# Cross-attention of a perceiver layer on one core: scores in two passes over the key columns, queries turned in 32 x 32 blocks by VectorE and spread by ScalarE, context in two banks

## The chip, the core and the metric

One core of one Trainium2 chip runs the whole kernel as one launch. Its engines are TensorE (PE in the views; its weight loads are PEld), VectorE (DVE), ScalarE (ACT), GpSimd (POOL) and SyncE (SP, which here only issues DMAs). The metric is device time in microseconds. Before the change it is 833.94 us, the median of three runs (831.2 to 836.29).

## The reference, cut to what matters

The layer has a cross-attention, a self-attention with relative positions, and a block with a second self-attention and a mixture of experts. The change touches the first alone. With x of 16 batches x 64 queries x 512 features, and 1,601 keys a batch, all in fp32:

```
h = layernorm(x)                                   # per query row, no scale or shift
scores  = einsum('bsh,bqh->bsq', ctx, h)           # 1601 keys x 64 queries
context = einsum('bsq,bsh->bqh', softmax(scores, axis=1), ctx)
y = x + context
```

## The kernel before

**Tiles.** The 16 batches are done two at a time, in `NT` = 8 tiles of 128 rows (64 queries of each of two batches; `b` is 0 or 1). The keys of a batch lie in `nat[k % 2]` with keys in the partitions, as 12 full groups of 128 and a tail of 65 (`JM` = 12, `TAIL` = 65, `JT` = 13). `nat` has two buffers, so the keys of tile k + 2 are loaded over those of tile k, in four pieces (`PIECES`: groups 0 to 3, 4 to 7, 8 to 11, the tail). SyncE issues each when a semaphore `context_part` says that the context product no longer needs the old ones (L476).

**Scores.** The product needs features in the partitions, on both sides. VectorE turns the keys in blocks of 32 x 32 (`columns`, L1808) into `ctxT`: partition group i of 32 holds keys 32i to 32i + 31 of each 128-key group, and the 512 features are 16 blocks `j`. A tile has two parts, `PARTS`: key groups 0 to 7 (`h` = 0, 8 turns of 128 x 1024) and 8 to 12 (`h` = 1, 8 turns of 128 x 640). Each turn counts `columns_ready` up. `scores(k)` (L583) then runs, for each of 16 blocks j, for both batches and all four partition groups, one product of 32 rows, 64 columns of queries and up to 416 keys (`KEYS_IN`), accumulated over j into PSUM banks 0 to 3 (`scores4`). In fp32 a product is two matmul instructions with a weight load each: 256 matmuls and 256 loads a tile. It waits chunk by chunk (`c`) for `columns_ready` of the second part of the keys.

**Queries.** As each partition group needs all queries, ScalarE writes the normed row four times over (`queries`, L1391, 128 x 2048 into `qn`), TensorE transposes it in 16 products (`query_transposes`, L548), four to a bank (`QUERY_BANK`), and ScalarE copies the four banks into `q4` (`query_columns_out`, L1396). This is woven into the previous tile's work.

**Softmax and context.** VectorE takes maxima (`maxima`, L1797), ScalarE exponentials (`exps`, L1400) into `prob`, TensorE transposes them (`prob_transposes`, 13 for a tile in four fills f, into `PROB_BANK`), VectorE copies fill 0 out and ScalarE fills 1 to 3 (`probs_out`). `context(k, f)` (L611) multiplies them with `nat`, f for f, all into bank 7: 16 matmuls for f below 3, four for the tail. VectorE's `finish` (L1853) scales bank 7 and adds it to y, and the next tile's context waits for it (`y1_ready`).

**Order.** It is written by hand, on each engine. On TensorE (L636 to L659) one turn of the loop is: scores(k), context(k-1, 2 and 3), prob_transposes(k, 0), query_transposes(k+1, 0), prob_transposes(k, 1), query_transposes(k+1, 1 and 2), context(k, 0), query_transposes(k+1, 3), prob_transposes(k, 2), context(k, 1), prob_transposes(k, 3). On VectorE (L1884 to L1898): maxima(k), first chunk of the next keys, finish(k-1), copy of fill 0, chunks 1 to 3, statistics for the later norm, denominators, the second part of the keys, then the first norm of tile k + 2 (`first_norm`: one statistic over 512 features and 15 small instructions). On ScalarE (L1436 to L1450): exponentials, the copies out, then `queries(k + 2)`.

Tile 0 is different: its keys 8 to 11 go through TensorE's transposes (`plain_key_transposes`, `plain_scores`), its score product has at most 288 columns (`FIRST_KEYS`), and its pieces are loaded in an order of their own (`load_first`, L452).

Of the kernel before, what the change touches and what calls it, by code (L numbers as in the profile page):

```python
# [17 lines left out]
P = 128  # L18
# [13 lines left out]
PROB_BANK = [4, 5, 4, 6]  # L32
# [10 lines left out]
PARTS = [(0, 8), (8, JT)]  # L43
NG, GB, NH, F, SEQ = 8, 8, 8, 128, 16
# [84 lines left out]
def perceiver_kernel(nc, x, ctx_keys, consts, vecs, rows, Wq, Wv, Wr, Wout, Wkvd, Wqd, Wku, Wqu, Wvu, Wropeq, Wropek,  # L129
                     Wo, Wexp, Wrouter, out):  # L130
    with ExitStack() as ctx:
# [60 lines left out]
        scope.close()  # L192

# [219 lines left out]
        def evicted(k):  # L413

            return 4 * k + (1 + HC if k > 0 else 0)
# [24 lines left out]
        def _(sp):  # L440
# [11 lines left out]
            def load_first():  # L452
# [5 lines left out]
                sp.dma_start(y[:, 1, :], x[P:2 * P, :]).then_inc(x_loaded[0], 16)  # L458
# [12 lines left out]
            sp.dma_start(y[:, 2:NT, :], x[2 * P:TOK, :].rearrange("(k p) d -> p k d", p=P)).then_inc(x_loaded[1], 16)  # L471
# [7 lines left out]
            sp.wait_ge(context_part, 3 * (NT - 1))  # L479
# [67 lines left out]
        def _(pe):  # L547
            def query_transposes(k, f):  # L548
                pe.wait_ge(qn_ready, k + 1)
                if f == 2:  # L550
                    pe.wait_ge(qt_act, evicted(k) + 1)
                elif k == 1 and f == 3:
                    pe.wait_ge(qt_act, evicted(1) + 2)
                elif k > 1 and f == 1:
                    pe.wait_ge(probT_dve, k)
                elif k > 1 and f == 3:
                    pe.wait_ge(probT_act, 3 * (k - 1) + 1)
# [25 lines left out]
            def scores(k):  # L583
                pe.wait_ge(qt_act, evicted(k) + 4)
                keys_in = FIRST_KEYS if k == 0 else KEYS_IN
                for c in range(HC):
                    pe.wait_ge(columns_ready, FIRST_COLUMNS + 16 * (k - 1) + 8 + 2 * c + 2 if k > 0 else 3 + HC + 2 + 2 * c + 2)
                    for j in range(4 * c, 4 * c + 4):
                        for b in range(2):
                            for i in range(4):  # L590
                                rows_i = slice(B32 * i, B32 * (i + 1))
                                last = nc.tensor.matmul(scores4[64 * b:64 * b + 64, i, 0:keys_in[i]],  # L592
                                                        q4[rows_i, j, 64 * b:64 * b + 64],
                                                        ctxT[rows_i, b, j, 0:keys_in[i]], start=j == 0, stop=j == NB - 1,
                                                        skip_group_check=True)
                last.then_inc(scores_full, 1)

            def prob_transposes(k, f):
# [3 lines left out]
                elif f >= 2 and k < NT - 1:  # L602
                    pe.wait_ge(qt_act, evicted(k + 1) + f)
                elif f == 2:
                    pe.wait_ge(probT_dve, k + 1)
                for j in range(4 * f, min(4 * f + 4, JT)):
# [4 lines left out]
            def context(k, f):  # L611
                if f == 0:
                    pe.wait_ge(probT_dve, k + 1)
                    if k > 0:
                        pe.wait_ge(y1_ready, k)
                    else:
                        pe.wait_ge(prob_ready, 3)
# [4 lines left out]
                for j in range(4 * f, min(4 * f + 4, JT)):  # L622
                    n = P if j < JM else TAIL
                    for b in range(2):
                        last = nc.tensor.matmul(bank[7][64 * b:64 * b + 64, :], probT[0:n, j, 64 * b:64 * b + 64],  # L625
                                                nat[k % 2][0:n, b, j, :], start=j == 0, stop=j == JT - 1,
                                                skip_group_check=True)
                if f != 2:
                    last.then_inc(context_part, 1)
# [6 lines left out]
            for k in range(NT - 1):  # L636
                scores(k)
                if k > 0:
                    context(k - 1, 2)
                    context(k - 1, 3)  # L640
                if k == 0:
# [3 lines left out]
                if k > 0:  # L645
                    query_transposes(k + 1, 0)
                prob_transposes(k, 1)
                if k > 0:
                    query_transposes(k + 1, 1)
                    query_transposes(k + 1, 2)  # L650
                context(k, 0)
                if k > 0:
                    query_transposes(k + 1, 3)
                prob_transposes(k, 2)
                context(k, 1)
                prob_transposes(k, 3)
# [4 lines left out]
            def norm_transposes(k):  # L661

                pe.wait_ge(hn_ready, k + 1)
                if k == 1:
# [725 lines left out]
        def _(act):  # L1390
# [4 lines left out]

            def query_columns_out(k, f):  # L1396
# [3 lines left out]
            def exps(k):  # L1400
                act.wait_ge(nmax_ready, k + 1)
                keys_in = FIRST_KEYS if k == 0 else KEYS_IN
# [33 lines left out]
            for k in range(NT - 1):  # L1436
# [4 lines left out]
                if k > 0:  # L1441
                    query_columns_out(k + 1, 0)
                probs_out(k, 1)
                if k > 0:
                    for f in range(1, 4):
                        query_columns_out(k + 1, f)
                probs_out(k, 2)
                probs_out(k, 3)
                if k + 2 < NT:
                    queries(k + 2)  # L1450
# [318 lines left out]
        def _(dve):  # L1769
# [44 lines left out]
            def first_columns():  # L1814
# [21 lines left out]
                first_factors(1, 2)  # L1836
# [16 lines left out]
            def finish(k):  # L1853

                dve.wait_ge(context_part, 3 * (k + 1))
                dve.scalar_tensor_tensor(y[:, k, :], bank[7][:], rinv[:, 0:1], y[:, k, :], ALU.mult,
# [26 lines left out]
            first_columns()  # L1883
            for k in range(NT - 1):  # L1884
                maxima(k)
                keys_columns(k + 1, 0, (0,))
                if k > 0:
                    finish(k - 1)
                probs_out(k)
                keys_columns(k + 1, 0, (1, 2, 3))  # L1890
                if k > 0:
                    second_stats(k - 1)
                denominators(k)
# [3 lines left out]
                if k + 2 < NT:  # L1897
                    first_norm(k + 2, k + 3)  # L1898
# [37 lines left out]
            dve.wait_ge(qt_full, turns(NT - 1) + 4)  # L1936
# [566 lines left out]
```

## Time and profile before

| | |
|---|---|
| median of three runs | 833.94 us |
| profiled execution | 833.91 us, span 832.1 us |
| granted TensorE clock, mean | 0.993 |
| PE busy (matmuls) | 793.4 us, 95% |
| PEld busy (weight loads) | 582.3 us |
| DVE, ACT, POOL busy | 521.0, 311.5, 301.2 us |
| read from and written to HBM | 102.0 and 24.2 MB, 152 GB/s over the span |

Busy time of an engine is the union of its instructions; matmuls overlap each other and their ends are modelled, so the chain of waits, which gives each moment to one instruction, is the better measure of what a group costs. "issue" in a view is idle time that ended with no semaphore the profile can name. The queue called "instruction" in the list of DMA queues carries the engines' own code.

### The profile page before, as it was taken

The numbers are of one execution on the slowest core, as the hardware profiler recorded it, in microseconds if no ns is written. First come the engines' busy times: TensorE is split into PE (matmuls) and PEld (weight loads), VectorE is DVE, ScalarE is ACT, GpSimd is POOL, SyncE is SP. The second block draws the span as 40 slices with busy tenths as digits, with TensorE's granted clock in tenths as the row PEclk, the third lists the DMA queues.
The fourth block names the chain that finished last, engine by engine and source line by source line (L and its number), as shares of the span: only waits on it lengthen the run. The fifth ranks groups of instructions, "written<-read, shape, count | busy, mean of one in ns | idle before, by whom it ended". The sixth has DMA issues, their size and how long they took to land.

```text
span 832.1 us, 16698 instructions
## 1 busy us (share of the span) xinstructions
PE 793.4 (95%) x6401; PEld 582.3 (70%) x6415; DVE 521.0 (63%) x1175; ACT 311.5 (37%) x827; POOL 301.2 (36%) x154
## 2 busy tenths in 40 slices
PE   4899999999999998989999999899999999999996
PEld 4555455545557777877877777688888888888883
DVE  5779777987754436576788888864473443343334
ACT  4312332333253428752257665723413111211211
POOL 0000000000162933543022221343639999994033
PEclk9999999999999999999999999999999999999999
DMA  9968555865502022021169100040476554541147
GB/s 348 378 229 315 199 210 229 317 227 204 215 21 83 1 60 96 2 87 48 52 232 384 44 0 0 2 152 1 163 259 215 172 202 151 175 152 50 53 117 259
DMA packets 46572, 127.00 MB, mean 153 GB/s; under 512 B 4000, under 2 KB 8352, under 8 KB 40368
## 3 DMA queue, kind: packets, MB, share of 16 engines
q1 hardware_dynamic: 36752, 105.44, 34.9%
q10 hardware_dynamic: 7200, 12.32, 4.2%
q0 software_dynamic: 2560, 8.39, 3.1%
q8 instruction: 44, 0.72, 0.4%
q14 instruction: 16, 0.13, 0.0%
HBM read 101.99 MB, written 24.15 MB: 152 GB/s over the span
## 4 chain that ended last, share of the span: by engine, by line
PE 78%; DVE 8%; ACT 3%; DMA 3%; issue 3%; POOL 2%; SPq 0%; another core or an unknown queue 0%; DVEq 0%; ACTq 0%; POOLq 0%
PE scores L592 11%; PE bank L625 11%; PE bank L1126 7%; PE bank L1128 7%; PE bank L1127 6%; ACT sp L1613 2%; PE bank L805 2%; PE bank L682 2%; PE bank L840 2%; POOL picked L1366 2%; PE bank L684 2%; PE bank L683 2%; PE bank L559 2%; PE bank L870 2%; PE bank L928 2%
## 5 line engine op out<-in xcount | busy, mean ns | idle before, releaser
L1812 DVE STREAM_TRANSPOSE ctxT<-nat 128x1024 f32<-128x1024 f32 (+3 forms) x124 | 116.8, 1005 | 2.2 <-DMA nat<-in_ctx_keys 2.0
L625 PE MATMUL bank<-nat,probT 128*64 128x512 f32 (+1 forms) x416 | 96.0, 606 | 0.1
L592 PE MATMUL scores<-ctxT,hn 32*64 32x385 f32 (+5 forms) x2048 | 88.4, 487 | 2.6 <-DVE ctxT L1812 1.3
L1233 POOL TENSOR_TENSOR wq_lo<-wq_raw,wq_hi 128x1024 fp32r<-128x1024 f32 x4 | 9.5, 2405 | 223.4 <-ACT wq_hi L1457 223.4
L1353 POOL TENSOR_TENSOR ring_lo<-ring_raw,ring_hi 128x2048 fp32r<-128x2048 f32 x18 | 83.0, 4612 | 15.1 <-ACT ring_hi L1700 14.0
L592 PEld LDWEIGHTS scores<-ctxT,hn 32*64 32x64 f32 x2048 | 62.0, 131 | 25.9 <-issue 16.4
L1126 PE MATMUL bank<-ring_hi,xg_lo 128*128 x180 | 74.2, 412 | 0.4 <-DVE xg_lo L2432 0.4
L1128 PE MATMUL bank<-ring_hi,xg_hi 128*128 x180 | 70.6, 392 | 0.0
L1127 PE MATMUL bank<-ring_lo,xg_hi 128*128 x180 | 70.1, 390 | 0.0
L625 PEld LDWEIGHTS bank<-nat,probT 128*64 128x64 f32 (+1 forms) x416 | 29.5, 138 | 53.8 <-issue 52.5
L2444 DVE TENSOR_TENSOR rhm_lo<-bank,rhm_hi 128x512 fp32r<-128x512 f32 x21 | 14.5, 692 | 79.5 <-ACT rhm_hi L1711 75.9
L1717 ACT COPY hn<-bank 128x512 f32<-128x512 f32 x22 | 12.9, 587 | 114.5 <-PE bank L1128 101.6
L1351 POOL TENSOR_TENSOR ring_hi<-ring_raw,cst 128x2048 fp32r<-128x2048 f32 x15 | 54.1, 3605 | 0.0
L1613 ACT ACTIVATE sp<-bank,s_bias 128x64 f32<-128x64 f32 x128 | 38.2, 327 | 21.6 <-DVE s_bias L2155 21.5
L1285 POOL TENSOR_TENSOR sp<-sp,s_inv 128x512 f32<-128x512 f32 x16 | 16.8, 1052 | 80.2 <-DVE s_inv L2161 80.2
L1128 PEld LDWEIGHTS bank<-ring_hi,xg_hi 128*128 128x128 f32 x180 | 33.8, 188 | 7.7
L1393 ACT ACTIVATE qn<-y,nmr,rstd 128x2048 f32<-128x2048 f32 x8 | 16.8, 2094 | 59.1 <-DVE nmr L1874 59.1
L2427 DVE TENSOR_SCALAR xg_hi<-bank,vec 128x128 fp32r<-128x128 f32 x88 | 24.8, 345 | 21.8 <-PE bank L1136 21.5
L1126 PEld LDWEIGHTS bank<-ring_hi,xg_lo 128*128 128x128 f32 x180 | 33.9, 188 | 6.3 <-issue 0.6
L1127 PEld LDWEIGHTS bank<-ring_lo,xg_hi 128*128 128x128 f32 x180 | 34.0, 189 | 5.9
L1366 POOL DMA_INDIRECT picked<-y_slots,slots x16 | 15.8, 987 | 50.4 <-POOLq L1360 44.1
L1126 PE MATMUL bank<-ring_hi,rhm_lo 128*128 x84 | 32.8, 390 | 0.0
(310 smaller groups left out, 1879.8 us busy)
## 6 DMA issues: line engine op xcount, KB each, us to landing
nat<-in_ctx_keys SPq DMA_DIRECT2D x48, 1024.0 KB, 7.3
ring_raw<-in_Wexp SPq DMA_DIRECT2D x21, 1024.0 KB, 6.3
x_slots<-zeros SPq DMA_DIRECT2D x1, 5632.0 KB, 17.7
y_slots<-zeros SPq DMA_DIRECT2D x1, 5632.0 KB, 32.4
hn<-x_slots ACTq DMA_DIRECT2D x22, 256.0 KB, 4.3
y_slots<-hn ACTq DMA_DIRECT2D x22, 256.0 KB
w_raw<-in_Wexp SPq DMA_DIRECT2D x3, 1024.0 KB, 5.7
nat<-in_ctx_keys SPq DMA_DIRECT2D x16, 130.0 KB
```

Source lines behind the costliest of these rows:

```text
L592: last = nc.tensor.matmul(scores4[64 * b:64 * b + 64, i, 0:keys_in[i]], q4[rows_i, j, 64 * b:64 * b + 64], ctxT[rows_i, b, j, 0:keys_in[i] ...
L625: last = nc.tensor.matmul(bank[7][64 * b:64 * b + 64, :], probT[0:n, j, 64 * b:64 * b + 64], nat[k % 2][0:n, b, j, :], start=j == 0, stop= ...
L1126: nc.tensor.matmul(b[:], x_lo[:, c, :], hi, start=c == 0, stop=False)
L1127: nc.tensor.matmul(b[:], x_hi[:, c, :], lo, start=False, stop=False)
L1128: last = nc.tensor.matmul(b[:], x_hi[:, c, :], hi, start=False, stop=c == HC - 1)
L1285: nc.gpsimd.tensor_tensor(sp_[par][:, at, :], sp_[par][:, at, :], s_inv[par][:, at].unsqueeze(2).broadcast_to([P, 8, SQ]), ALU.mult).then_ ...
L1351: nc.gpsimd.tensor_tensor(ring_hi[at], ring_raw[at], zero, ALU.add).then_inc(split_hi, 1)
L1353: last = nc.gpsimd.tensor_tensor(ring_lo[at], ring_raw[at], ring_hi.bitcast(F32)[at], ALU.subtract)
L1366: nc.gpsimd.indirect_dma_start(picked[2 * k + i][:], None, y_slots, bass.IndirectOffsetOnAxis(slots[:, k, i:i + 1], 0)).then_inc(picked_lo ...
L1613: last = nc.scalar.activation(sp_[par][:, h, :], bank[4 + f][:, n * SQ:(n + 1) * SQ], ACT.Exp, bias=s_bias[par][:, h:h + 1], scale=SELF_SCALE,
L1812: dve.transpose(dst, src).then_inc(columns_ready, 1)
L2427: last = dve.tensor_scalar(xg_hi[par][:, c, :], columns[c], weights[c], None, ALU.mult)
```

## The change

TensorE's query transposes go for tiles 2 to 7. ScalarE writes the normed row once (128 x 512, into the first four groups of `prob`, which is free between two tiles), VectorE turns it in 32 x 32 blocks into the next four, and ScalarE copies each 32-partition block g to each partition group i, 16 copies, into `q4` for odd tiles and the memory of `qn` for even ones. `scores` runs over the key columns in two passes: all 16 blocks j for keys of the first part (256 columns for each group), then all 16 for the second (up to 160); each pass waits for its own part of the key turns. Tile 0 keeps one pass, tiles 0 and 1 keep the old queries. Context goes into bank 6 for even tiles and bank 7 for odd ones, and `context_part` counts each of four fills. TensorE's turn of the loop becomes scores(k), context(k-1, 2), prob_transposes(k, 0 and 1), context(k-1, 3), context(k, 0), prob_transposes(k, 2 and 3), context(k, 1). The norm arithmetic moves from once a tile to batches (`NORMED` and `TURNED` are the counts of `norm_ready` to wait for).

```diff
-PROB_BANK = [4, 5, 4, 6]
+PROB_BANK = [4, 5, 4, 5]
+NORMED = {2: 2, 3: 4, 4: 4, 5: 4, 6: 7, 7: 7}
+TURNED = {2: 3, 3: 5, 4: 6, 5: 8, 6: 9, 7: 10}
...
+        qn_rows = prob[:, 0:HC, :].rearrange("p t (j a) -> p (t j) a", a=B32)
+        q_blocks = prob[:, HC:2 * HC, :].rearrange("p t (j e) -> p (t j) e", e=B32)
+        q_even = qn[:].rearrange("p j r a -> p j (r a)")
...
+        def queries_of(k):
+
+            return q_even if k > 1 and k % 2 == 0 else q4
+
+        def context_bank(k):
+
+            return bank[7 if k % 2 else 6]
...
-                sp.dma_start(y[:, 1, :], x[P:2 * P, :]).then_inc(x_loaded[0], 16)
+                sp.dma_start(y[:, 1:3, :], x[P:3 * P, :].rearrange("(k p) d -> p k d", p=P)).then_inc(x_loaded[0], 16)
...
                 for p, (j0, j1) in enumerate(PIECES):
-                    sp.wait_ge(context_part, 3 * k + min(p, 2) + 1)
+                    sp.wait_ge(context_part, P_FILLS * k + p + 1)
                     load_piece(k + 2, k % 2, j0, j1)
...
             def scores(k):
-                pe.wait_ge(qt_act, evicted(k) + 4)
...
+                pe.wait_ge(qt_act, evicted(k) + (4 if k < 2 else 1))
+                queries = queries_of(k)
+                early = PARTS[0][1] * B32
+                parts = [[(0, n) for n in FIRST_KEYS]] if k == 0 else [[(0, early)] * 4, [(early, n) for n in KEYS_IN]]
+                for h, keys_in in enumerate(parts):
+                    for c in range(HC):
+                        pe.wait_ge(columns_ready, FIRST_COLUMNS + 16 * (k - 1) + 8 * h + 2 * c + 2 if k > 0 else 3 + HC + 2 + 2 * c + 2)
+                        for j in range(4 * c, 4 * c + 4):
+                            for b in range(2):
+                                for i in range(4):
+                                    rows_i, at = slice(B32 * i, B32 * (i + 1)), slice(*keys_in[i])
+                                    last = nc.tensor.matmul(scores4[64 * b:64 * b + 64, i, at],
+                                                            queries[rows_i, j, 64 * b:64 * b + 64], ctxT[rows_i, b, j, at],
+                                                            start=j == 0, stop=j == NB - 1, skip_group_check=True)
                 last.then_inc(scores_full, 1)
...
             def context(k, f):
                 if f == 0:
                     pe.wait_ge(probT_dve, k + 1)
-                    if k > 0:
-                        pe.wait_ge(y1_ready, k)
-                    else:
-                        pe.wait_ge(prob_ready, 3)
+                    if k > 1:
+                        pe.wait_ge(y1_ready, k - 1)
...
+            def spread_queries(k):
+                act.wait_ge(norm_ready, NORMED[k])
+                nc.scalar.activation(qn_rows, y[:, k, :].rearrange("p (j a) -> p j a", a=B32), ACT.Identity,
+                                     bias=nmr[:, k:k + 1], scale=rstd[:, k:k + 1]).then_inc(qn_ready, 1)
+                act.wait_ge(norm_ready, TURNED[k])
+                for g in range(4):
+                    for i in range(4):
+                        last = nc.scalar.copy(queries_of(k)[B32 * i:B32 * (i + 1), :, B32 * g:B32 * (g + 1)],
+                                              q_blocks[B32 * g:B32 * (g + 1)])
+                last.then_inc(qt_act, 1)
...
+            def turn_queries(k):
+                dve.wait_ge(qn_ready, k + 1)
+                dve.transpose(q_blocks, qn_rows).then_inc(norm_ready, 1)
+
             for k in range(NT - 1):
                 maxima(k)
                 keys_columns(k + 1, 0, (0,))
+                probs_out(k)
                 if k > 0:
                     finish(k - 1)
-                probs_out(k)
-                keys_columns(k + 1, 0, (1, 2, 3))
+                denominators(k)
+                keys_columns(k + 1, 0, (1, 2))
+                if k + 2 < NT:
+                    turn_queries(k + 2)
+                keys_columns(k + 1, 0, (3,))
                 if k > 0:
                     second_stats(k - 1)
-                denominators(k)
                 keys_columns(k + 1, 1, range(HC))
                 if k == 0:
                     dve.wait_ge(x_loaded[1], 3 * 16)
-                if k + 2 < NT:
-                    first_norm(k + 2, k + 3)
+                    first_norm(3, 6)
+                if k == 1:
+                    first_stats(6, NT)
+                elif k == 2:
+                    first_factors(6, NT)
```

On ScalarE the loop's end is `spread_queries(k + 2)` in place of `queries(k + 2)`, and `exps(k)` for k from 1 to 6 also waits for the spread queries of tile k + 1 (`qt_act`), as they are read out of `prob`.

## Rows read from the trace of the kernel before

**Rows 1.** the page of the whole run: busy us; the granted clock in tenths

```profile
PE 793.4 (95%) x6401; PEld 582.3 (70%) x6415; DVE 521.0 (63%) x1175; ACT 311.5 (37%) x827; POOL 301.2 (36%) x154
...
PEclk9999999999999999999999999999999999999999
```

**Rows 2.** the chain of waits, 0 to 240 us: start, us, what

```profile
76.22 11.35 PE scores L592 x234
...
92.59 0.44 PE bank L559 x4
...
93.55 1.06 PE bank L559 x8
...
98.20 0.59 PE bank L559 x4
...
103.06 11.35 PE scores L592 x236
```

**Rows 3.** the chain of waits, 84 to 132 us

```profile
120.19 8.81 DMA nat<-in_ctx_keys
...
129.09 1.58 DVE ctxT L1812 x2
```

**Rows 4.** timeline of VectorE, 84 to 136 us: start, us, idle before

```profile
101.05 5.93 DVE L1812 STREAM_TRANSPOSE ctxT<-nat 128x640 f32<-128x640 f32 x8
...
114.53 1.03 DVE L1800 TENSOR_REDUCE mx<-scores 128x2 f32<-128x832 f32 x1 [4.07 <-PE scores L592]
```

**Rows 5.** timeline of ScalarE, 84 to 136 us

```profile
116.71 0.69 ACT L1408 ACTIVATE prob<-scores,nmax 128x512 f32<-128x512 f32 x1 [4.12 <-DVE nmax L1806]
```

**Rows 6.** timeline of PE, 23 to 31.5 us, with idle before

```profile
24.46 5.09 PE L592 MATMUL scores<-ctxT,hn 32*64 32x288 f32 x155 [0.41 <-DVE ctxT L1812]
30.81 0.98 PE L592 MATMUL scores<-ctxT,hn 32*64 32x288 f32 x24 [1.26 <-issue]
```

**Rows 7.** stage table: window, us, busy (x instructions) of PE, PEld, DVE, ACT, POOL

```profile
0.00:29.20 29.20, 17.93 (x219) 14.12 (x220) 18.88 (x44) 9.30 (x12) 2.04 (x6) 1.00 0.95 369
...
0.00:110.30 110.30, 95.79 (x1229) 57.94 (x1236) 85.21 (x172) 33.91 (x66) 2.04 (x6) 0.98 0.79 299
```

**Rows 8.** DMA queues, 28.2 to 29.4 us: packets, MB, share

```profile
q8 instruction: 1, 0.02, 5.3%
```

**Rows 9.** DMA queues, 34.5 to 35.6 us

```profile
q8 instruction: 1, 0.02, 5.8%
```

**Rows 10.** DMA queues, 102.99 to 210.4 us, four tiles

```profile
q8 instruction: 11, 0.18, 0.7%
```

**Rows 11.** DMA queues, 110.8 to 112.3 us

```profile
q8 instruction: 1, 0.02, 5.2%
```

**Rows 12.** stage table; the last three: clock, DMA share, GB/s

```profile
104.00:105.00 1.00, 1.00 (x34) 0.77 (x25) 1.00 (x3) 0.00 (x0) 0.00 (x0) 1.00 1.07 442
...
110.00:111.00 1.00, 1.00 (x34) 0.71 (x24) 0.39 (x3) 0.50 (x1) 0.00 (x0) 1.00 0.29 98
...
39.40:42.80 3.40, 3.36 (x8) 1.79 (x10) 3.40 (x4) 0.90 (x5) 0.00 (x0) 0.52 0.97 336
```

**Rows 13.** line L592, 30.5 to 34.4 us: duration, first and last start

```profile
L592 PE MATMUL scores<-ctxT,hn x101: 374/401/452, 30.8 to 33.8; 32*64 32x288 f32 x49, 32*64 32x257 f32 x26, 32*64 32x256 f32 x26
```

**Rows 14.** line L592, 102.9 to 114.4 us

```profile
L592 PE MATMUL scores<-ctxT,hn x256: 481/507/558, 103.0 to 113.9; 32*64 32x416 f32 x61, 32*64 32x385 f32 x49, 32*64 32x384 f32 x18
```

**Rows 15.** line L787, 302 to 303 us

```profile
L787 PE MATMUL bank<-kT,ku_g x64: 196/196/217, 302.1 to 302.7; 128*32 128x32 f32 x64
```

**Rows 16.** ScalarE by shape, 0 to 215 us: busy us, mean ns

```profile
L1377 ACT COPY hn<-bank 128x512 f32<-128x512 f32 x32 | 18.0, 587 | 29.5 <-PE bank L559 29.1
...
L1408 ACT ACTIVATE prob<-scores,nmax 128x512 f32<-128x512 f32 x20 | 13.5, 685 | 25.2 <-DVE nmax L1806 25.2
...
L404 ACT COPY prob<-hn 32x512 f32<-32x512 f32 x2 | 1.2, 618 | 0.0
```

**Rows 17.** VectorE by shape, 0 to 215 us: busy us, mean ns

```profile
L1812 DVE STREAM_TRANSPOSE ctxT<-nat 128x512 f32<-128x512 f32 x10 | 6.2, 679 | 0.0
```

More of the change, by code:

```diff
@@ L413, in evicted @@
         def evicted(k):
-            return 4 * k + (1 + HC if k > 0 else 0)
+            return 4 * min(k, 2) + (1 + HC if k > 0 else 0) + max(k - 2, 0)
+        def queries_of(k):
+            return q_even if k > 1 and k % 2 == 0 else q4
+        def context_bank(k):
+            return bank[7 if k % 2 else 6]
         def plain_keys(b, c):
@@ L583, in scores @@
             def scores(k):
-                pe.wait_ge(qt_act, evicted(k) + 4)
[L585 to L595, printed above, removed]
+                pe.wait_ge(qt_act, evicted(k) + (4 if k < 2 else 1))
[12 more added lines that the diff above has]
+                                                            start=j == 0, stop=j == NB - 1, skip_group_check=True)
                 last.then_inc(scores_full, 1)
@@ L601, in prob_transposes @@
                     pe.wait_ge(qt_act, evicted(1) + 4)
-                elif f >= 2 and k < NT - 1:
-                    pe.wait_ge(qt_act, evicted(k + 1) + f)
                 elif f == 2:
                     pe.wait_ge(probT_dve, k + 1)
+                elif f == 3 and k < NT - 1:
+                    pe.wait_ge(probT_act, 3 * k + 1)
                 for j in range(4 * f, min(4 * f + 4, JT)):
@@ L624, in context @@
                     for b in range(2):
-                        last = nc.tensor.matmul(bank[7][64 * b:64 * b + 64, :], probT[0:n, j, 64 * b:64 * b + 64],
+                        last = nc.tensor.matmul(context_bank(k)[64 * b:64 * b + 64, :], probT[0:n, j, 64 * b:64 * b + 64],
                                                 nat[k % 2][0:n, b, j, :], start=j == 0, stop=j == JT - 1,
                                                 skip_group_check=True)
-                if f != 2:
-                    last.then_inc(context_part, 1)
+                last.then_inc(context_part, 1)
             pe.wait_ge(cst_loaded, 16)
@@ L639, in _ @@
                     context(k - 1, 2)
-                    context(k - 1, 3)
-                if k == 0:
+                else:
                     for f in range(4):
@@ L644, in _ @@
                 prob_transposes(k, 0)
-                if k > 0:
-                    query_transposes(k + 1, 0)
                 prob_transposes(k, 1)
                 if k > 0:
-                    query_transposes(k + 1, 1)
-                    query_transposes(k + 1, 2)
+                    context(k - 1, 3)
                 context(k, 0)
-                if k > 0:
-                    query_transposes(k + 1, 3)
                 prob_transposes(k, 2)
+                prob_transposes(k, 3)
                 context(k, 1)
-                prob_transposes(k, 3)
             context(NT - 2, 2)
@@ L1401, in exps @@
                 act.wait_ge(nmax_ready, k + 1)
+                if 0 < k < NT - 1:
+                    act.wait_ge(qt_act, evicted(k + 1) + 1)
                 keys_in = FIRST_KEYS if k == 0 else KEYS_IN
@@ L1440, in _ @@
                 exps(k)
[L1441 to L1448, printed above, removed]
+                for f in range(1, P_FILLS):
+                    probs_out(k, f)
                 if k + 2 < NT:
-                    queries(k + 2)
+                    spread_queries(k + 2)
             def weight_high(hi, raw, loaded, pieces=range(HC)):
@@ L1835, in first_columns @@
                         columns(0, b, 4 * c, 4 * c + 4, 4, 8)
-                first_factors(1, 2)
+                first_stats(2, 3)
+                first_factors(1, 3)
             def keys_columns(k, h, chunks):
@@ L1935, in _ @@
             dve.tensor_copy(ident_bf[:], ident).then_inc(consts_cast, 1)
-            dve.wait_ge(qt_full, turns(NT - 1) + 4)
+            dve.wait_ge(scores_full, NT - 1)
             for k in range(4):
```

14 lines of the change are left out of this document (5 added, 9 removed).

## The prediction

> **What bounds the kernel now.** The page of the whole run comes first: TensorE is busy for 793.4 of 832.1 us at the full granted clock [rows 1]. The cross-attention fills the first 230 us, in eight tiles. In the chain of waits one steady tile is TensorE from end to end: the score product of tile 2 starts at 76.22, that of tile 3 at 103.06, so a tile takes 26.84 us, and the chain names no other engine in between. The score product has 11.35 us of it, and the sixteen query transposes have 0.44 + 1.06 + 0.59 = 2.09 us in three pieces [rows 2]. Once, at tile 4, a load of keys stands on the chain and VectorE turns keys late (129.09); TensorE loses about 1 us there [rows 3]. VectorE turns the second part of the keys in 5.93 us from 101.05, is idle for 4.07 us before it takes the next maxima at 114.53, so it has room [rows 4]. ScalarE's exponentials start at 116.71 after an idle time of 4.12 us [rows 5].
>
> One more row decides this case. In tile 0 the score product stops for 1.26 us with no releaser ("issue") and goes on at 30.81 [rows 6], while VectorE's last needed key turn is long over. By then 219 matmuls and 220 weight loads had run [rows 7]. In the same stretch the queue named "instruction" delivers one packet of 0.02 MB, which at 5.3% of 16 engines in a 1.2 us window took 1.0 us [rows 8]; the next one starts after 34.5 [rows 9]. Over four steady tiles there are 11 such packets [rows 10] for 4 x (256 + 52 + 13 + 16) = 1,348 matmuls and as many loads, some 245 of these per packet and some waits beside them. From the first stop to 110.3 us, 1229 + 1236 - 439 = 2,026 more had run [rows 7], eight times 253, and a packet starts at 110.8 to 110.9 [rows 11]. I read this as: TensorE's instructions come in blocks of 256, two blocks are held, a block is asked for when the one before the last is used up, and whoever uses a block faster than the next one arrives stands still.
>
> **Price of a block.** Under full DMA load: from the restart at 30.81, where the next block can be asked for, to its packet at about 34.5 is 3.7 us, its transfer 1.0, and 1.5 us lie between the first packet's end (about 29.3) and the restart. That is 6.2 us; I use 6.0. The DMA engines are full in the first 7 us of a score product (share 1.07 at 104 us) and nearly idle after it (0.29 at 110 us) [rows 12]. Idle: 0.6 us from the count at 110.3 to the packet at 110.9, 1.25 for the transfer (5.2% of 16 engines in 1.5 us) [rows 11], and 1.5 again is 3.4; with a sequencer that reads 1.4 us ahead of the array it is 4.8. I use 3.6, near the lower end, since the 1.5 was measured under load. Before the change 256 instructions of a score product last 5.6 us, less than 6.0, and yet no stop shows in 11.35 us, so the sequencer does read ahead; I allow it 0.8 us once per product.
>
> **The change, part by part.**
>
> *Two passes.* Each score slot of eight products costs two cycles of 2.4 GHz per key column: after the restart 100 starts lie in 3.0 us, 0.24 us a slot, for 288 columns [rows 13], and 255 starts in 10.9 us for 416 [rows 14]. Pass one has 256 columns (0.216 us), pass two 160 (0.136 us): 32 x 0.352 = 11.3 us against 11.2. Streaming costs +0.1 us a tile, +0.7 for seven. A slot of pass two holds eight loads and eight products in 136 ns. Line L787 starts 64 products with their loads in about 0.6 us, 9 ns a pair, so eight need 75 ns [rows 15] and that floor isn't reached. The Trainium skill, "TensorE: Matmul & The Clock Gate", Back-to-back issue gap, gives the smallest matmuls an issue floor of 25 ns each; were it the floor of each of the eight, a slot of pass two would last 200 ns and the tile 2.0 us longer, which the L787 row contradicts.
>
> *Instructions.* The change doubles the score product's instructions, from 512 to 1,024 a tile. In pass one a block lasts 16 x 0.216 = 3.5 us and in pass two 2.2 us, against arrivals of 6.0 and 3.6. With the first border in the middle of a block the product takes 1.7 us to it, then 6.0, 3.6 and 3.6 for three blocks, 1.1 for the remaining 128, less 0.8: 15.2 us against 11.45. That is +3.7 us a tile, **+26 us** for tiles 1 to 7. Bounds: nothing at all if blocks come in time; with 6.2, 4.8 and 4.8 it is +6.3 a tile, +44 us.
>
> *Query transposes.* For tiles 2 to 7 they leave TensorE: 6 x 2.09 = **-12.5 us** [rows 2]. All else on its chain stays (20 context products, 13 transposes, 32 context products), only in another order. The first probability transpose now follows 16 products (3.58 us) after the scores and not 20 (4.47). The first exponential is done 2.2 + 0.7 = 2.9 us after they end [rows 5], so 0.7 us of cover is left; without it tile time would grow by what it is late.
>
> *What takes their place.* ScalarE loses per tile four copies of 0.587 and the spread of 2.09 us, gains one activation of about 0.69 and sixteen copies of 32 x 512 at 0.618 = 9.9 us [rows 16]. The copies start when VectorE has turned the block, some 12 us after the scores end, and are done by 22; the next exponentials need ScalarE at 27. Five microseconds are left. VectorE gains one turn of 0.68 us [rows 17], which waits for ScalarE's activation (behind its last probability copy, at about 11 us) when VectorE arrives, at about 11 us too. Behind it queue the last chunk of the first key part and the second part; pass one needs the former three quarters in, with 2 to 5 us to spare. The norm arithmetic of 3.4 us a tile goes from the loop's end into batches. All of this I cost at nothing; ScalarE and VectorE stay under 80% busy.
>
> *Waits and transfers.* Key turns of the second part are now needed 7 us later, and SyncE releases the third load after 16 context products, not after 20: the stop at 129 us goes, **-1 us**. Two context banks take a wait away that is met anyway (VectorE has finished the tile before long since): 0. The load of x for tiles 1 and 2 is one of 512 KB ahead of key pieces, and statistics of tile 2 stand before tile 1's factor: 256 KB at some 400 GB/s, **+0.3 us** (0 to 0.6). SyncE issues as many transfers as before.
>
> Sum: 26 - 12.5 + 0.7 - 1 + 0.3 = +13.5, less 1 because borders that fall just outside a product cost nothing: +12.5. The profiled execution took 833.9 us (span 832.1), and so did the median. Forecast: **846.4 us**.
>
> **The rivals.** *Blocks arrive in time.* 833.9 - 12.5 + 0.7 - 1 + 0.3 = 821.4 us. For it: in 210 us only one stop has this look. The Trainium skill, "Runtime: NRT & Kernel Launch", Instruction fetch mechanics, describes refills in blocks of 256 instructions and calls the crossing mostly hidden, with 2,048 instructions held for TensorE; by that page this rival would be the result. The stop after 439 counted instructions speaks against it. Chance 0.25. *Blocks arrive late by half as much*, +13 and not +26: 833.9 ± 3. It holds if a block takes 5.6 us loaded and 2.8 idle. Chance 0.15. *The throttle joins in.* After a stretch with gaps TensorE was granted 0.52 of its clock, 1.2 in place of 2.4 GHz, in 39.4 to 42.8 us [rows 12]; stops of 2 us in a product could bring such stretches, each with a loss of 0.48 x 3.4 = 1.6 us, one in each of seven tiles: +11.5, 858 us. Chance 0.10. *ScalarE becomes the bound*: if a spreading copy took over 0.93 us rather than 0.62, the exponentials would come late; at 1.2 us, 4 us in six tiles, on either of the above: 846 without late blocks. Chance 0.05. What remains, 0.45, is the forecast as it stands.
>
> **The numbers.** About 0.5%, 4 us, is what a measurement of this kernel can tell from no change. Slower: 0.45 + 0.10 + 0.05 and little of the middle case, 0.61. Same: 0.12. Faster: 0.25 and a little, 0.27. Likeliest case's own range: 838 to 860. With the case of no late blocks inside, and the upper bound cut where the throttle case ends: 820 to 862.
>
> **What would show it.** Right: score line with 4,096 - 256 matmuls; stops marked "issue" in the middle of score products, longest in pass two; products of 14 to 17 us; three or four instruction packets in each. Query transposes down to 32, sixteen copies a tile hidden. Wrong: score products of 11.4 us and a tile of 24.8, which is the first rival; or idle TensorE before exponentials or behind VectorE's turns, which is the last one.

## The result, and the profile after

The changed kernel takes 856.42 us (median of four, 851.27 to 860.32), beside 833.72 us (831.2 to 836.29) for the kernel before in the same session: ratio 1.0252, interval 1.0214 to 1.029, some 21 us slower. The forecast was 846.4 us and "slower"; the time lies in the range. The profiled execution is the slowest of the four, 860.32 us with a span of 858.5, 26.4 us over the span before.

The page of the changed kernel: busy time by engine, the instruction queue, the chain, and the groups of the score line and of its neighbours (shape, count, busy and mean ns, idle before and its releaser).

```profile
span 858.5 us, 20111 instructions
PE 793.6 (92%) x8110; PEld 593.8 (69%) x8111; DVE 514.6 (60%) x1125; ACT 348.3 (41%) x899; POOL 300.8 (35%) x154
...
q8 instruction: 57, 0.93, 0.4%
...
PE 81%; DVE 7%; issue 5%; DMA 2%; POOL 2%; ACT 2%; another core or an unknown queue 0%; SPq 0%; DVEq 0%; ACTq 0%; POOLq 0%
...
L604 PE MATMUL scores<-ctxT,hn 32*64 32x256 f32 (+5 forms) x2304 | 61.2, 354 | 17.4 <-issue 17.0
...
L604 PE MATMUL scores<-ctxT,qn 32*64 32x256 f32 (+3 forms) x1536 | 36.8, 334 | 11.9 <-issue 11.9
```

TensorE is busy for as long as before (793.6 against 793.4 us [rows 1]) while the span has grown: the idle time has grown by 26.2 us. As the query transposes (12.5 us) have left TensorE and its busy time has not fallen, about as much busy time was added elsewhere; it is found below. The score line (L604 now) has 2,304 + 1,536 = 3,840 matmuls. Idle time ahead of them is put down to "issue", 17.0 + 11.9 us, which is no semaphore of any engine. There was one such stop, in tile 0 [rows 6]. Now there are 18.

The waits of TensorE in the first 260 us (waited for: us, times, longest), after:

```profile
PE scores L604 <- issue: 28.8, 18, 3.0
...
PE scores L604 <- DVE ctxT L1821: 0.4, 1, 0.4
```

The timeline of TensorE after, tiles 2, 4 and 7 (start us, us, tiles, count, idle before), shows where the stops lie; the first line is the end of the context products ahead of one. In what follows a restart is the moment at which TensorE goes on after a stop, and a border is the place in the program where one block of instructions ends and the next begins.

```profile
75.47 3.65 PE L634 MATMUL bank<-nat,probT 128*64 128x512 f32 x16
79.06 4.54 PE L604 MATMUL scores<-ctxT,qn 32*64 32x256 f32 x152
84.96 3.51 PE L604 MATMUL scores<-ctxT,qn 32*64 32x256 f32 x128 [1.36 <-issue]
90.07 2.42 PE L604 MATMUL scores<-ctxT,qn 32*64 32x160 f32 x128 [1.60 <-issue]
93.81 2.12 PE L604 MATMUL scores<-ctxT,qn 32*64 32x160 f32 x104 [1.32 <-issue]
...
139.78 7.66 PE L604 MATMUL scores<-ctxT,qn 32*64 32x256 f32 x274
150.01 2.43 PE L604 MATMUL scores<-ctxT,qn 32*64 32x160 f32 x128 [2.57 <-issue]
153.75 2.14 PE L604 MATMUL scores<-ctxT,qn 32*64 32x160 f32 x110 [1.30 <-issue]
...
231.68 5.40 PE L604 MATMUL scores<-ctxT,hn 32*64 32x256 f32 x181
238.92 3.24 PE L604 MATMUL scores<-ctxT,hn 32*64 32x256 f32 x128 [1.85 <-issue]
245.12 5.32 PE L604 MATMUL scores<-ctxT,hn 32*64 32x129 f32 x203 [2.96 <-issue]
```

The pieces between two stops have exactly 128 matmuls, each with its weight load: 256 instructions. Between restarts lie 6.2 us (238.92 to 245.12), 5.1 us (84.96 to 90.07) and 3.74 us (90.07 to 93.81; 150.01 to 153.75); this is the price of a block. The stage table of the same stretches (window, us, busy of each engine, granted clock, DMA share, GB/s) tells what sets them apart:

```profile
79.00:85.00 6.00, 4.64 (x159) 3.58 (x158) 6.00 (x9) 5.88 (x11) 0.00 (x0) 1.00 1.00 414
85.00:90.00 5.00, 3.47 (x128) 3.25 (x128) 2.55 (x4) 2.75 (x5) 0.00 (x0) 1.00 0.48 198
90.00:96.00 6.00, 4.61 (x234) 4.13 (x235) 0.00 (x1) 0.00 (x0) 0.00 (x0) 1.00 0.03 5
121.60:126.50 4.90, 4.87 (x173) 4.65 (x173) 0.00 (x0) 0.00 (x0) 0.00 (x0) 0.65 0.02 3
...
238.90:245.10 6.20, 3.24 (x128) 2.95 (x128) 1.97 (x5) 3.89 (x4) 3.25 (x2) 0.97 0.90 355
245.10:250.50 5.40, 5.38 (x204) 5.01 (x204) 0.00 (x0) 0.00 (x0) 5.40 (x3) 0.72 0.05 14
```

With the DMA engines at a share of 0.90 a block costs 6.2 us, at 0.48 it costs 5.1, at 0.03 it costs 3.7. In two products (tiles 3 and 7) TensorE's granted clock was also at its lower level for part of the window (0.50 from 122.2 to 125 us, and from 245.1 to 248 us), which gives the means of 0.65 and 0.72.

**Where the 26.4 us come from.** Score products of tiles 1 to 7 in the chain of waits last 16.35, 16.80, 17.26, 16.03, 15.90, 15.64 and 18.75 us, 116.7 together against 79.6 in the chain of before: +37.1, of which 27.5 are the 17 stops. Between two products lie 13.34 us (65.79 to 79.13) against 15.50 (the chain of before has the end of product 1 at 60.72 and the start of product 2 at 76.22 [rows 2]); over the six stretches that is -13.1, with the wait at tile 4 left out. That wait, for the load of keys [rows 3], is gone: the stretch there was 16.40 us long and not 15.50, so -0.9. The start gives +0.1. Product 7 thus ends at 250.50 and not at 227.33, +23.2, and what follows takes 608.0 us and not 604.8: +3.2. The 9.6 us by which the products grew beyond their stops and these 3.2 are the added busy time.

The other engines stayed hidden. ScalarE's timeline after, tile 3:

```profile
106.24 0.82 ACT L1400 ACTIVATE prob<-y,nmr,rstd 128x512 f32<-128x512 f32 x1
107.89 10.03 ACT L1405 COPY qn<-prob 32x512 f32<-32x512 f32 x16 [0.83 <-DVE prob L1896]
128.78 0.69 ACT L1423 ACTIVATE prob<-scores,nmax 128x512 f32<-128x512 f32 x1 [10.85 <-DVE nmax L1815]
```

The sixteen copies end at 117.9, and ScalarE then idles 10.85 us until the next maxima. Some 5.9 us of that room are there only because the product became longer (17.26 us for 11.35).

### The profile page after: what moved, and what is told of

It reads as the page before. It is cut to its first block, busy times and chain, and to the rows that moved or that the text cites. A ratio compares the mean times of both kernels' runs of the same rounds, so it can differ in the third digit from the quotient of the medians.

```text
span 858.5 us, 20111 instructions
## 1 busy us (share of the span) xinstructions
PE 793.6 (92%) x8110; PEld 593.8 (69%) x8111; DVE 514.6 (60%) x1125; ACT 348.3 (41%) x899; POOL 300.8 (35%) x154
## 4 chain that ended last, share of the span: by engine, by line
PE 81%; DVE 7%; issue 5%; DMA 2%; POOL 2%; ACT 2%; another core or an unknown queue 0%; SPq 0%; DVEq 0%; ACTq 0%; POOLq 0%
PE scores L604 11%; PE bank L634 11%; PE bank L1128 6%; PE bank L1130 6%; PE bank L1129 6%; PE bank L836 2%; PE bank L807 2%; PE bank L837 2%; PE bank L684 2%; POOL picked L1368 2%; PE bank L686 2%; PE bank L842 2%; PE bank L685 2%; PE bank L872 2%; PE bank L619 2%
## 5 line engine op out<-in xcount | busy, mean ns | idle before, releaser
L604 PE MATMUL scores<-ctxT,hn 32*64 32x256 f32 (+5 forms) x2304 | 61.2, 354 | 17.4 <-issue 17.0
L604 PEld LDWEIGHTS scores<-ctxT,hn 32*64 32x64 f32 x2304 | 52.0, 138 | 29.1 <-issue 25.5
L604 PE MATMUL scores<-ctxT,qn 32*64 32x256 f32 (+3 forms) x1536 | 36.8, 334 | 11.9 <-issue 11.9
L604 PEld LDWEIGHTS scores<-ctxT,qn 32*64 32x64 f32 x1536 | 32.3, 131 | 18.0 <-issue 16.4
L1809 DVE TENSOR_REDUCE mx<-scores 128x2 f32<-128x832 f32 (+1 forms) x8 | 7.9, 991 | 59.1 <-PE scores L604 59.1
L1423 ACT ACTIVATE prob<-scores,nmax 128x512 f32<-128x512 f32 x23 | 15.5, 684 | 67.8 <-DVE nmax L1815 67.8
```

The lines of the kernel that those rows point to most:

```text
L604: last = nc.tensor.matmul(scores4[64 * b:64 * b + 64, i, at], queries[rows_i, j, 64 * b:64 * b + 64], ctxT[rows_i, b, j, at], start=j == 0 ...
```

## The experiments

**One pass, all else kept.**

```
parts = [[(0, n) for n in (FIRST_KEYS if k == 0 else KEYS_IN)]]
pe.wait_ge(columns_ready, FIRST_COLUMNS + 16 * (k - 1) + 8 + 2 * c + 2 ...)
```

> The changed kernel with its score product put back into one pass over the keys; spread queries, two context banks and the new order stay. Theory (instruction blocks of 256 arrive too slowly for 1,024 short instructions a tile): no stop marked issue inside a score product of tiles 1 to 7, products of 11.4 us where they are not waiting, 37 us less in all. But one pass must wait for the second part of the key turns, which VectorE has 16.2 us after the scores of the tile before, while TensorE's other work now lasts 13.3: 2.9 us of waiting at the start of six or seven products, named as VectorE's. Sum 856 - 37 + 18 = 837 us, 832 to 841. Rival (the spreading copies, the banks or the order cost the time): above 850 us, with the stops still there.

Measured: 839.77 us, ratio 1.0107 (1.0045 to 1.0169). The waits of this kernel, 0 to 260 us:

```profile
PE scores L604 <- DVE ctxT L1821: 18.6, 7, 3.0
...
PE scores L604 <- issue: 1.0, 1, 1.0
```

The stops for instructions in tiles 1 to 7 are gone. In their place stands a wait for key turns in tiles 1 to 6 (17.6 of the 18.6 us; 1.0 is in tile 0): the tile without its query transposes is shorter than VectorE's queue, and a single pass needs all columns of a block at once. Two products in the chain of this kernel, tiles 2 and 4:

```profile
75.66 11.43 PE scores L604 x224
...
131.26 13.11 PE scores L604 x235
```

Four of the seven products last 11.4 us again. Tiles 4, 5 and 6 take 13.11, 14.34 and 14.34 us, at a mean granted clock of 0.87, 0.79 and 0.79, each behind a wait of 3.0 us; the expectation had no term for that. Tiles 2 and 3 had the same wait and kept the full clock. The seven products come to 87.5 us, 29.2 less than in the changed kernel, and the waits take 17.6 back: 11.6 us, beside 12 by the ratios (1.0252 and 1.0107). So the two passes did buy something, the waits for VectorE, but at a price of 37.1 us; low clock cost the products 7.5 us with one pass and 3.3 with two.

**Two passes alone, in the kernel before.** Only the loop over column ranges was brought in; the query transposes stay on TensorE.

```
+ for h, keys_in in enumerate(parts):
      for c in range(HC):
-         pe.wait_ge(columns_ready, ...)
+         pe.wait_ge(columns_ready, FIRST_COLUMNS + 16 * (k - 1) + 8 * h + 2 * c + 2 ...)
```

> The kernel before with nothing but the score product in two passes. Theory of the blocks: seven score products of 15.5 to 18.5 us with two or three stops each, as in the changed kernel, and nothing won elsewhere but the 1 us wait at tile 4: 833.7 + 37 - 1 = 870 us, 862 to 875. Rival (two passes are harmless by themselves and something else of the change costs): 831 to 836 us.

Measured: 863.42 us, ratio 1.0399 (1.0327 to 1.0471). Against the changed kernel's 1.0252 this is 1.47% of 834, 12 us with some 7 either way by the two intervals: what the rest of the change gave back. The chains agree: between two products lie 15.50 us here (126.02 to 141.52) and 13.34 in the changed kernel, which is the query transposes. Its waits:

```profile
PE scores L594 <- issue: 25.9, 19, 3.1
```

A product in its timeline:

```profile
78.74 7.39 PE L594 MATMUL scores<-ctxT,hn 32*64 32x256 f32 x262
87.81 2.43 PE L594 MATMUL scores<-ctxT,hn 32*64 32x128 f32 x128 [1.67 <-issue]
91.81 2.40 PE L594 MATMUL scores<-ctxT,hn 32*64 32x128 f32 x122 [1.58 <-issue]
```

The stops come with the doubled instructions, whatever ScalarE, the banks or the turn order do.

**Few key loads.** The blocks were thought late because their reads stand behind the bulk loads. Here the keys of tiles 2 to 7 are loaded for one partition of 128, so the output comes from old keys; every instruction stays.

```
+ if k > 1:
+     dst, src = dst[0:1], src[0:1]
```

> The changed kernel in which the keys of tiles 2 to 7 are loaded for 1 of 128 partitions alone, so those tiles compute with keys of tiles 0 and 1; every instruction stays. Theory of the blocks, with a price of 6.0 us under DMA load and 3.6 idle: a block in pass one lasts 3.5 us and now arrives in 3.6, so the stops in pass one go nearly all, those of 1.3 us in pass two stay; products of 14 to 15 us, in all 12 to 19 us less than the changed kernel: 837 to 844. Rival one (a floor of the array or of the sequencer for short matmuls): products still 15.6 to 18.8 us, 856. Rival two (contention with key loads is all of it): products of 11.4 us, 818 to 823.

Measured: 834.52 us (830.09 to 837.11), ratio 1.0033, 2.5 us below the expected range, and in the profile 12.1 us of stops for 28.8 (its waits, then its timeline in tile 3):

```profile
PE scores L607 <- issue: 12.1, 11, 3.0
```

```profile
98.72 8.75 PE L607 MATMUL scores<-ctxT,hn 32*64 32x256 f32 x341
107.86 2.43 PE L607 MATMUL scores<-ctxT,hn 32*64 32x129 f32 x128 [0.39 <-issue]
111.32 1.04 PE L607 MATMUL scores<-ctxT,hn 32*64 32x129 f32 x43 [1.02 <-issue]
```

Pass one, where a block lasts 3.46 us of streaming, doesn't stop in tiles 1 to 6 once the DMA engines are idle (the first stop comes after 335 matmuls at the earliest, and pass one has 256); pass two, where it lasts 2.18, still does, and its restarts are 107.86 to 111.32 = 3.46 us apart. The products of these tiles last 12.4 to 13.6 us, not the 14 to 15 that were expected, hence the miss. Tile 7, which shares the DMA engines with the weights of the next stage, keeps stops of 1.55 and 2.96 us. As a control, the same few loads in the kernel before:

> The kernel before with the keys of tiles 2 to 7 loaded for 1 of 128 partitions: the control to the changed kernel without those loads, which gained 22 us. Theory of the blocks: 256 instructions of a score product last 5.6 us here and no block is late in either case, so only the 1 us wait at tile 4 goes: 829 to 834 us, products of 11.3 us. Rival (key loads slow the products themselves): products shorter than 11.3, 10 us or more off.

Measured: 832.22 us, ratio 0.9986 (0.9962 to 1.001). The bulk loads cost the kernel before nothing and the changed one some 20 us.

**Context products between the passes.** If time apart from a score product lets the blocks catch up, then sixteen context products between the two passes should save a block per tile.

```
  for h, keys_in in enumerate(parts):
+     if h == 1:
+         between()                    # the caller gives context(k - 1, 1)
...
-     context(k, 1)                    # at the end of the loop over k
```

> The changed kernel with the second quarter of the context product, 16 matmuls and 16 loads of 3.6 us in all, moved from before the score product to between its two passes, for tiles 1 to 6. The same instructions, the same streaming. Theory of the blocks: 32 instructions take 3.6 us there, so the block asked for in pass one arrives behind them, and about one stop a tile (1.3 to 2.5 us) goes: six times 2, less up to 3 for keys that are now loaded later: 840 to 850 us, faster than the changed kernel. Rival (a floor for short matmuls, or the passes' own cost): the same 852 to 860 us as the changed kernel, since the work is only moved.

Measured: 864.0 us, ratio 1.0385. The expectation failed: stops are 30.2 us in 14 places, against 28.8 in 18. The timeline of this kernel in tile 5:

```profile
171.44 6.29 PE L606 MATMUL scores<-ctxT,hn 32*64 32x256 f32 x223
179.45 1.23 PE L606 MATMUL scores<-ctxT,hn 32*64 32x256 f32 x33 [1.72 <-issue]
180.62 3.65 PE L636 MATMUL bank<-nat,probT 128*64 128x512 f32 x16
184.20 3.78 PE L606 MATMUL scores<-ctxT,hn 32*64 32x160 f32 x207
191.45 1.90 PE L606 MATMUL scores<-ctxT,hn 32*64 32x128 f32 x49 [3.47 <-issue]
```

Pass two now has one stop and not two, but of 3.47 us. The moved products also release the key buffers later, so the load falls into pass two (DMA share 0.73 and then 0.84 from 184.2 to 191.45 us, 0.02 in the last blocks of the changed kernel), where a block lasts only 2.2 us. By tile it went both ways: in tiles 2, 4 and 6 the stops fell by 1.2 to 1.9 us each, in tiles 1, 3 and 5 they grew by 1.1 to 2.1, and in tile 7 by 1.2. Twice, at 154.12 and 219.27 us, a load of keys was 8.32 us of the chain. And the granted clock was lower: up to the end of product 7, which comes 11.0 us later than in the changed kernel, the stretches at the lower level cost 10.2 us and not 5.1 (the time, times one less the granted clock). I had allowed 3 us for the later keys, and nothing for what their transfer does to the blocks beside it. To tell the two apart, the same move with few loads:

> The changed kernel without the key loads, and with 16 context matmuls between the passes. In the version with all loads this cost 8 us and did not gain, and there the load of keys that the moved work sets free ran in pass two, so that blocks in it came at the loaded price. Without loads the theory of the blocks gives back one stop a tile of 0.4 to 1.4 us: 12 us of stops fall to 6 or less, 825 to 832 us against 834.5. Rival (short matmuls have a cost of their own, or order is no matter): 834 to 836 us with 12 us of stops.

Measured: 833.17 us, ratio 0.9984. Stops are 10.3 us in 8 places, and outside tiles 0 and 7 they fell from 6.3 us (few loads) to 2.7: the catching up works when no load collides with it. The time as a whole missed its range by 1 us. In the profile product 7 ends 2.9 us earlier than with few loads (224.5 against 227.4 us), but what follows took 606.9 us and not 600.9. Those later stages are the same instructions; over all profiles they spread from 600.9 to 608.0 us, so the end of product 7 is the finer measure. Why they spread wasn't tried.

**Shifting the program.** If blocks have fixed borders in the program, waits added at its very start must move the stop of tile 0. The waits are on a semaphore that is already met.

```
- pe.wait_ge(cst_loaded, 16)
+ for _ in range(1 + 128):
+     pe.wait_ge(cst_loaded, 16)
```

> The kernel before with 128 more waits, all met already, at the start of TensorE's program, where it has nothing to do for 9 us. No matmul changes. Theory of the blocks: block borders move by 128 instructions, so the stop in tile 0 can no longer come after 219 matmuls; the border before it falls into the transposes of the keys at about 16 us, its successor is there by 23, and the next is asked for at about 27 us and needed at 34: the stop of 1.26 us at 29.6 us goes, or one shorter than 0.6 comes near 33 us. Rival (a wait for data or a DMA at that moment): the stop stays after 155 matmuls of the score product, at 29.6 us, with 1.2 to 1.3 us.

> The kernel before with 40 more waits at the start of TensorE's program. The run with 128 showed that two waits make one instruction, and the stop of tile 0 moved from after 155 matmuls of the score product to after 123, which is 64 instructions. Theory of the blocks: 40 waits are 20 instructions or 10 matmuls, so the stop comes after 145 matmuls. Rival (the stop is tied to a time or to data): after 155, or after 123 again.

One execution each, 836.5 and 831.37 us. Timelines of TensorE, first with 128 waits, then with 40:

```profile
22.85 4.12 PE L592 MATMUL scores<-ctxT,hn 32*64 32x288 f32 x123 [0.66 <-DVE ctxT L1813]
28.67 4.14 PE L592 MATMUL scores<-ctxT,hn 32*64 32x288 f32 x128 [1.70 <-issue]
34.88 0.65 PE L592 MATMUL scores<-ctxT,hn 32*64 32x288 f32 x5 [2.07 <-issue]
```

```profile
24.08 4.79 PE L592 MATMUL scores<-ctxT,hn 32*64 32x288 f32 x145 [0.41 <-DVE ctxT L1813]
30.33 3.64 PE L592 MATMUL scores<-ctxT,hn 32*64 32x288 f32 x111 [1.46 <-issue]
```

Before, the stop came after 155 matmuls [rows 6]. The 128 waits moved it to 123, by 32 matmuls with their loads or 64 instructions, so two waits take the room of one instruction; the second stop follows 128 matmuls later. I had expected 128 instructions and a product without a stop there, and that was wrong. With the size of a wait known, 40 of them had to move it by 20 instructions, 10 matmuls: it came after 145. Where a stop falls is a matter of the address in the program.

**One pass with interleaved key turns.** The 18.6 us of the first experiment are an order of VectorE's queue: it turned all blocks of the first key part before any of the second. Now both parts of block 0 and 1 come first.

```
TURN_ORDER = [(0, 0), (0, 1), (0, 2), (1, 0), (1, 1), (0, 3), (1, 2), (1, 3)]
  keys_columns(k + 1, 0, (1, 2))
+ keys_columns(k + 1, 1, (0, 1))
  turn_queries(k + 2)
  keys_columns(k + 1, 0, (3,))
+ keys_columns(k + 1, 1, (2, 3))
```

> The changed kernel with one pass, and VectorE's key turns in another order: chunks 0 and 1 of the second part of the keys before the turn of the queries and before chunk 3 of the first part, statistics last. Theory: the one-pass version waited 18.6 us in seven products for VectorE's turns, and for nothing else that was new; here chunk 0 is ready 12.9 us after the scores of the tile before and TensorE comes at 13.3, so these waits go, nothing stops inside a product, and what the change takes off TensorE (12.5 us of query transposes) remains: 817 to 825 us, faster than both. Rival (ScalarE's sixteen copies or the keys' transfers cost something that the two passes hid): 830 us or more.

Measured: 825.9 us (822.57 to 827.84), ratio 0.9905 (0.9875 to 0.9935), just above the expected range; the interval leaves no doubt that it is faster than the kernel before, by about 1%. Its waits, and after them its chain around tile 3:

```profile
PE scores L605 <- DVE ctxT L1822: 6.7, 6, 1.6
...
PE scores L605 <- issue: 1.1, 1, 1.1
```

```profile
88.61 0.33 SPq L464
...
88.98 6.72 DMA nat<-in_ctx_keys
...
95.73 1.58 DVE ctxT L1822 x2
...
97.45 11.49 PE scores L605 x219
```

Product 7 ends at 215.96 us, 11.4 before the 227.33 of before. Of these, 3.8 lie ahead of the product of tile 1 (start 45.51 against 49.30): there the profile of before has its stretch of low clock, with 16 context matmuls in 5.51 us at 39.44 us for 3.65 here, and this one has none up to product 7. The medians, 825.9 against 833.64 us, are 7.7 apart. What is left of the wait, about 1.1 us a tile, is a key load that starts when the context products have let its buffer go. Then the last four of those products were put ahead of the probability transposes, and VectorE's last step of the tile ahead of its copy:

> The interleaved version with the last piece of the context product (4 matmuls) right behind the third on TensorE, and VectorE's finish ahead of its copy. There six products still waited 6.7 us in all for VectorE's first turn of the second part of the keys, which waited for the transfer of the tail, issued 5.7 us after the scores of the tile before. Here it is issued 1.2 us earlier; theory: the wait of 1.1 us a tile goes to 0 to 0.5, against which the first copy of the transposed probabilities comes 0.5 us later and may hold the context product: 0 to 4 us less than the interleaved version's 825.9, so 822 to 826. Rival (the first 2 MB piece, not the tail, is what lands last): no change in the wait, 826 to 829 us.

Measured: 824.33 us (820.85 to 827.61), ratio 0.9901 (0.9873 to 0.9928). The wait for key turns is 5.5 us for 6.7, but 2.6 us of a new one stand beside it (TensorE for VectorE's copy of the transposed probabilities, six times), and the load on the chain at 88.12 us takes 8.07 us. The two cannot be told apart by their times.

## Why the prediction came out as it did

**Reading the instruction queue: right.** Blocks of 256, two held, asked for as the one before runs out. This was read from one stop of 1.26 us and a count of packets; pieces of exactly 128 matmuls and a stop that moves with the program's address show it. That two blocks are held, and not more, shows in the first stop of a product: in tiles 1, 2, 3, 5 and 7 it comes at the second border, one block after the first, though the context products before it use few instructions and leave time to fill a larger store. The rival "blocks in time" at 821.4 us is excluded, and the Trainium skill's rule behind it ("Runtime: NRT & Kernel Launch", Instruction fetch mechanics: crossings mostly hidden, 2,048 instructions held for TensorE) does not hold in this kernel: there are 17 stops in seven products, 256 instructions apart. The rival "late by half as much" is excluded by products that grew by 37.1 us and not by 13.

**The first block of a product: right, where it stopped.** Borders lie 128 matmuls before each stop. In tile 2 that is after 24 matmuls, at 0.65 us, and the restart comes at 5.83: 5.2 us, which is 6.0 less the 0.8 allowed. Tiles 3, 5, 1 and 7 give 5.2, 5.2, 5.5 and 5.7.

**The blocks behind it: mis-sized, and this is most of what was missed.** "In pass one a block lasts 3.5 us and in pass two 2.2 us, against arrivals of 6.0 and 3.6": I took each block after the first at the idle price. The idle price was right: 3.46 to 4.01 us between restarts at a DMA share of 0.05 or less. But in tiles 2 and 3 the load still took nearly half of the DMA engines (5.11 and 4.84 us at a share of 0.48 and 0.40), in tile 7 the weights of the next stage took nearly all (6.20), and in tiles 4 and 6, whose border fell 18 and 12 matmuls into the product, the first block was in time (a border at 3.94 us was passed without a stop where the rule has a restart at 5.69, 1.75 us saved) and the next one paid 6.2 and 6.0 us. Why it was in time isn't shown; my estimate is that a sequencer that reads ahead reaches a border so near the start while the slower context products still run (3.58 us for 16, 0.22 us a matmul, against 0.027), so that 0.8 us was too small an allowance there. Against 3.6 us these five are 1.5 + 1.2 + 2.6 and, net of what the free block saved, 0.9 + 0.6: 6.8 of the 11.4 us by which the products exceed the forecast. A product is +5.3 us and not +3.7. The upper bound of +44 for seven, from the same rows, held it.

**The allowance of 1 us for borders outside a product: wrong.** All seven products had two or three stops.

**The throttle: in part.** Two stretches fell into products, not seven. The last 171 matmuls of tile 3 took 4.89 us where 2.9 of streaming and 0.3 after a restart were due, the last 203 of tile 7 took 5.38 for 3.8: 1.6 to 1.7 us each, close to the 1.6 of that rival.

**Stops cost more than their idle time.** 27.5 us idle and 3.3 of throttle leave 6.3 of the +37.1, 0.37 us per stop, with 0.7 in all foreseen as streaming. A piece of 128 in pass two lasts 2.43 us where 16 slots are 2.18. My block price ran from restart to restart and so had this in it; it explains why the idle time alone falls short of the growth.

**Query transposes: right**, -13.1 for -12.5, with 12 us between two kernels by their ratios. **ScalarE and VectorE hidden: right**; the activation took 0.82 us for an estimated 0.69, a copy 0.616 for 0.618, and the rival with ScalarE as the bound did not occur. **The load at tile 4: right**, -0.9 for -1. **The start**: +0.1 for +0.3.

Put together on the profiled execution: 846.4, + 11.4 for products (37.1 against 26 + 0.7 - 1), - 0.6, + 0.1 and - 0.2 for the other terms, + 3.2 in the stages behind, which I had left at zero, is 860.3. The median lies 4 us below that profile, so the forecast missed the median by 10. That the stages behind took 3.2 us longer in this profile is not part of the mechanism: the same instructions spread by 7 us between profiles.

## What to carry to other kernels

A product that is split in two for the sake of an earlier start has twice the instructions; divide the time of 256 instructions (here 128 small matmuls with their loads, 2.2 to 3.5 us) by what a block of code takes to arrive (3.5 to 6.2 us here), and do it for the stretch in which bulk loads run. Before adding instructions to remove a wait for a producer, look at the order in which the producer works: the same wait went down from 18.6 to 6.7 us when the eight steps of key turns were put in another order, with no work added. When a step is moved, ask which transfer its semaphore releases and what that transfer will then run beside.

## What the runs showed that was not expected

- Reading code competes with data loads, and only a program near the limit shows it: the changed program is 1.0252 of before with the key loads and 1.0033 without most of them, while the kernel before doesn't notice (0.9986).
- The price of a block goes with the load: between restarts in tiles 1 to 7 lie 3.46 to 4.01 us at a DMA share of 0.05 or less and still 3.74 at 0.32, then 4.84 and 5.11 at 0.40 and 0.48, and 6.20 at 0.90. It is no straight line, and no run set the load by itself.
- Two repeated waits on a semaphore that is already met take the room of one instruction: 128 waits moved the stop by 64 instructions, 40 by 20.
- Short waits can cost clock as well: with one pass, three of seven products ran partly at the lower granted clock and lasted 13.11, 14.34 and 14.34 us for 11.4, and context products between the passes came with twice the loss of the changed kernel. Why some waits bring it and others of the same length don't wasn't tried.
- The last block border of tiles 3 and 7 passed without a stop. My reading, argued and not tried: while the clock was down, the 128 matmuls after the restart took some 3.8 us in tile 3 and 3.6 in tile 7, about as long as a block takes to arrive (3.5 to 3.7 us), so the low clock's 1.6 us there stand in place of a stop of some 1.3 us.
